# Filler work of an attention and MLP block put in another order within four slots

## The chip, the cores and the metric

The kernel runs on one core of one Trainium2 chip. The metric is the device time of one execution in microseconds. Three runs of the kernel before took 985.18, 988.05 and 989.5 us; their median is 988.05 us.

## The reference

For eight rows b of 512 tokens with 256 features the reference computes a transformer block in fp32. `x` is normalised and modulated (`h`). The attention is the sum of two paths: a light one on all tokens (layer norm, projections q, k, v of 8 heads of 64, each window of 64 tokens attending to itself and its two neighbours, output product `wo_l`), and a heavy one on 256 routed tokens:

```
idx = argsort(scores)                 # scores = h . rt_q and h . rt_kv
rq, rkv = the last 256 rows by each of the two orders
hq = rms(rq) @ wq_h ; hk, hv = split(rms(rkv) @ wkv_h)
ho = softmax(hq hk^T / 8) hv @ wo_h   # written back to the rows of rq
x = x + ga * (light_out + heavy_out)
h = layernorm(x) * (1 + cb) + sb
x = x + gb * spikes(square(relu(h @ W_fc^T)) @ W_proj^T)
```

`spikes` counts, over five steps of a leaky integrator, how often it fires; the kernel does this with five thresholds.

## The kernel before

Each engine has an instruction list written out by hand, and semaphores join them. The work is a pipeline over b = 0 to 7. An iteration has 24 slots: 16 of light attention (4 pairs of heads x 4 tiles of 128 queries) and 8 of heavy attention. In slot s TensorE issues `scores` for the attention step two ahead, then the filler units of the slot, then `turn` (four transposes of the probabilities of this slot) and `attend` for the slot before (lines 1074 to 1083). ScalarE does, in this order, the copy of the transposed probabilities, exp for the step two ahead, its share of the units, and the normalisation for the step one ahead (lines 848 to 860). VectorE copies out the step two back, inverts a row sum, takes the row minimum of the step two ahead, does its share of the units, and last the stages of the slot (lines 1380 to 1395). So on every engine the units come behind the softmax work of the slot. POOL (GpSimd) and SP (the queue that starts the direct DMAs) walk through the slots in the same way.

`SLOT_UNITS` (lines 59 to 84) says which filler units stand in which slot, in order. The units that matter here:

- HT r transposes the routed rows of order r (0: queries, 1: keys and values) into `hT`. ScalarE makes the high part with two activations (line 792), VectorE the low part with two subtractions (line 1318), and the last of these frees the bank.
- HO t is the output product of the heavy path of the row before, four matmuls for each of two tiles. It needs `hoT`, which VectorE completes in slot 1 (line 1300). VectorE multiplies the result by the gate (line 1335), SP stores it, and POOL gathers it back in the order of the tokens in slot 3 (line 635). VectorE adds these rows in slot 5 (line 1245), takes their statistics (lines 1251, 1256), POOL makes the root, and VectorE normalises in slot 6 (line 1264).
- Z3 k transposes the normalised rows; ScalarE modulates and frees the bank (line 776), VectorE splits the result into a high and a low part (lines 1227, 1230), which FC reads.
- HV t is the projection of the routed rows to v; VectorE copies it and frees the bank (line 1313). It is read first in slot 16.
- FC i and YA i are the two products of the MLP. RK r sums the comparisons to ranks (20 small matmuls), which VectorE casts (line 1326) and POOL's scatters read from slot 14 on. SR r transposes the router scores.
- Q, K, V, ZT, HQ, HK, LO and the N-units are further projections and transposes.

All units but YA write to `ps_unit`, which has two banks. They are given in turn, by the place of the unit in the list of its segment (lines 120 and 150 to 160):

```
BANKED = {s: [u for u in units if u[0] != "YA"] for s, units in SEGMENTS.items()}
    i = BANKED[segment].index(unit)
    bank, before = i % BANKS, i // BANKS
```

Before a unit is filled TensorE waits until the last use of its bank has been drained (`fill`, line 881). The segments are `first` (b = 0, without HO, Z3, FC and YA), `loop` (b = 1 to 6), `last` (b = 7, without ZT, SR, RK and the N-units) and a tail with its own list. Those of b = 1 to 6 are called full iterations here.

Of the kernel before, what the change touches and what calls it, by code (L numbers as in the profile page):

```python
# [57 lines left out]

SLOT_UNITS = {
    0: [("HT", 0), ("V", 3)],  # L60
    1: [("HO", 0), ("HO", 1)],
    2: [("HT", 1), ("Q", 2)],
    3: [("HV", 1)],
    4: [("K", 2)],
    5: [("Q", 3)],
    6: [("K", 3)],
    7: [("HV", 0), ("Z3", 0), ("Z3", 1)],
    8: [("FC", 0), ("FC", 1)],
    9: [("HQ", 0), ("FC", 2), ("YA", 0)],
    10: [("FC", 3), ("YA", 1), ("SR", 0)],  # L70
    11: [("FC", 4), ("YA", 2)],
    12: [("FC", 5), ("YA", 3), ("HK", 0)],
    13: [("RK", 0), ("FC", 6), ("YA", 4), ("SR", 1)],
    14: [("FC", 7), ("YA", 5)],
    15: [("YA", 6), ("ZT", 0)],
    16: [("YA", 7), ("ZT", 1), ("RK", 1)],
# [1440 lines left out]
```

## Time and profile before

| | |
|---|---|
| median of 3 runs | 988.05 us |
| profiled execution | 984.39 us |
| its span, first to last instruction | 982.7 us |
| TensorE matmuls busy | 879.1 us (89%) |
| ScalarE busy | 617.0 us (63%) |
| VectorE busy | 552.5 us (56%) |
| GpSimd busy | 402.6 us (41%) |
| mean granted TensorE clock | 0.969 |

The span lies within the time of the execution, which has 1.7 us around it. Busy shares are averages over the whole kernel. An engine that has nothing to do costs time only where another engine, in the end TensorE, waits for it.

### The profile page before, as it was taken

To read this page: it belongs to the slowest core of one execution; us is meant where nothing else is said; L and a number is where in the kernel's file an instruction comes from. 1 tells how busy PE (TensorE), PEld (TensorE's weight loads), DVE (VectorE), ACT (ScalarE), POOL (GpSimd) and SP (SyncE) were. 2 spreads that over 40 slices of the span, in tenths; PEclk is the share of its full clock that TensorE was granted. 3 is DMA by queue.
4 is the path that set the end of the run, shared out by engine and by line. 5 is a ranking of instruction groups with operands and counts; after the bars stand their busy time and mean duration, and the time that the engine had idled before them with its cause. 6 is when DMAs were issued, how large, how long until landed. Compare 5 with 4: busy or idle time off the path is not lost.

```text
span 982.7 us, 19077 instructions
## 1 busy us (share of the span) xinstructions
PE 879.1 (89%) x6866; PEld 674.1 (69%) x6866; DVE 552.5 (56%) x1556; ACT 617.0 (63%) x1682; POOL 402.6 (41%) x453
## 2 busy tenths in 40 slices
PE   5759689899998999899999999899999999999655
PEld 2436567678766877678766877678766877688455
DVE  7645644764557454764557464764557454613344
ACT  1167666676567766676567766676567766777332
POOL 4422040364525453364525453365525443252333
PEclk7989899999999999999999999999999999999968
DMA  9120002100220012200220012200220011200100
GB/s 320 67 81 1 25 31 70 60 1 13 68 84 23 1 39 86 59 2 12 74 79 22 2 38 87 60 2 12 76 76 23 2 38 55 60 2 1 39 22 22
DMA packets 32461, 45.06 MB, mean 46 GB/s; under 512 B 3928, under 2 KB 26720, under 8 KB 32368
## 3 DMA queue, kind: packets, MB, share of 16 engines
q1 hardware_dynamic: 26944, 31.24, 9.9%
q0 software_dynamic: 4608, 12.59, 3.9%
q8 instruction: 56, 0.92, 0.4%
q14 instruction: 37, 0.30, 0.1%
q10 hardware_dynamic: 816, 0.00, 0.0%
HBM read 28.85 MB, written 14.97 MB: 45 GB/s over the span
## 4 chain that ended last, share of the span: by engine, by line
PE 64%; DVE 21%; ACT 6%; issue 4%; POOL 2%; DMA 2%; SPq 1%; DVEq 0%; POOLq 0%; ACTq 0%
PE ps_unit L889 25%; PE ps_y L1000 9%; PE ps_oT L1069 7%; PE ps_unit L937 6%; PE ps_pT L1045 5%; PE ps_scores L1033 4%; PE ps_scores L1025 3%; DVE row_min L1289 3%; PE ps_unit L942 3%; ACT probs L828 3%; DVE late L1215 1%; DVE hT L1318 1%; DVE bn L1251 1%; ACT hT L792 1%; DVE hn L1264 1%
## 5 line engine op out<-in xcount | busy, mean ns | idle before, releaser
L828 ACT ACTIVATE probs<-ps_scores,row_min 128x256 f32<-128x256 f32 (+1 forms) x384 | 171.9, 453 | 133.7 <-DVE row_min L1289 133.6
L839 ACT ACTIVATE probs<-probs,row_inv 128x256 f32<-128x256 f32 (+1 forms) x384 | 166.1, 485 | 0.0
L846 ACT ACTIVATE probsT<-ps_pT 128x512 f32<-128x512 f32 x192 | 113.5, 591 | 41.7 <-PE ps_oT L1069 41.7
L1289 DVE TENSOR_REDUCE row_min<-ps_scores 128x2 f32<-128x384 f32 (+1 forms) x192 | 122.3, 637 | 23.6 <-PE ps_scores L1033 10.8
L1045 PE MATMUL ps_pT<-ident,probs 128*128 128x128 f32 x768 | 116.4, 274 | 3.1 <-ACT probsT L846 2.9
L889 PE MATMUL ps_unit<-xT,wfcT 128*128 128x512 f32 (+1 forms) x432 | 106.1, 386 | 7.3 <-DVE xT L1230 6.7
L889 PE MATMUL ps_unit<-xT,wqkv 128*128 128x512 f32 x384 | 108.6, 419 | 4.0 <-POOL xT L651 4.0
L1300 DVE COPY loT<-ps_oT 128x128 f32<-128x128 f32 x128 | 36.3, 283 | 132.2 <-PE ps_oT L1069 132.2
L428 POOL TENSOR_TENSOR hid<-hid 128x512 f32<-128x512 f32 (+1 forms) x64 | 63.3, 989 | 107.9 <-ACT hid L805 106.9
L1045 PEld LDWEIGHTS ps_pT<-ident,probs 128*128 128x128 f32 x768 | 93.0, 141 | 19.3 <-issue 3.5
L1000 PEld LDWEIGHTS ps_y<-wprojT,hid_parts 128*128 128x128 f32 x768 | 99.8, 191 | 9.1 <-issue 5.2
L1000 PE MATMUL ps_y<-wprojT,hid_parts 128*128 128x256 f32 x768 | 105.2, 285 | 0.2
L889 PEld LDWEIGHTS ps_unit<-xT,wfcT 128*128 128x128 f32 x432 | 73.6, 194 | 29.3 <-issue 17.7
L574 POOL TENSOR_SCALAR veps<-mv 128x4 f32<-128x4 f32 (+1 forms) x25 | 5.1, 204 | 215.1 <-DVE mv L1147 125.0
L889 PEld LDWEIGHTS ps_unit<-xT,wqkv 128*128 128x128 f32 x384 | 70.7, 191 | 24.9 <-issue 10.9
L432 POOL TENSOR_TENSOR hid_parts<-hid,hid_parts 128x512 fp32r<-128x512 f32 (+1 forms) x64 | 78.1, 1220 | 22.0 <-ACT hid_parts L809 20.4
L1069 PE MATMUL ps_oT<-probsT,v 128*64 128x128 f32 x1024 | 85.5, 288 | 0.1
L615 POOL DMA_INDIRECT sorted_rows<-hn,rank x64 | 65.4, 1022 | 44.3 <-DVE rank L1326 31.7
L1025 PE MATMUL ps_scores<-kT,qT 64*64 64x192 f32 (+1 forms) x1024 | 71.3, 336 | 6.7 <-ACT probs L828 5.6
L828 ACT ACTIVATION_READ_ACCUMULATOR probs<-ps_scores,row_min 128x1 f32 x384 | 75.8, 197 | 0.0
L1069 PEld LDWEIGHTS ps_oT<-probsT,v 128*64 128x64 f32 x1024 | 54.2, 137 | 22.0 <-issue 22.0
L809 ACT ACTIVATE hid_parts<-hid 128x512 fp32r<-128x512 f32 (+1 forms) x72 | 42.0, 584 | 42.5 <-PE ps_y L1000 42.0
(157 smaller groups left out, 1508.6 us busy)
## 6 DMA issues: line engine op xcount, KB each, us to landing
xa<-in_L_attn_x SPq DMA_DIRECT2D x8, 512.0 KB, 4.9
routed<-sorted_rows SPq DMA_DIRECT2D x16, 256.0 KB, 2.9
lx<-in_L_attn_x SPq DMA_DIRECT2D x8, 512.0 KB, 3.9
out_x<-spikes SPq DMA_DIRECT2D x16, 256.0 KB, 2.9
routed_out<-late SPq DMA_DIRECT2D x8, 256.0 KB, 2.1
full<-mod_rows SPq DMA_DIRECT2D x7, 256.0 KB, 5.0
sorted_rows<-hn,rank POOLq DMA_INDIRECT x64, 2.4
gate_a<-mod_rows SPq DMA_DIRECT2D x8, 128.0 KB, 3.5
```

The lines of the kernel that those rows point to most:

```text
L428: eng.tensor_tensor(square, hid_relu[:, i % 2, cols], hid_relu[:, i % 2, cols], ALU.mult).then_inc(squared, 1)
L432: eng.tensor_tensor(hid_parts[1][:, i % 2, cols], square, hid_parts[0][:, i % 2, cols].bitcast(F32), ALU.subtract).then_inc(low, 1)
L615: pool.indirect_dma_start(out=sorted_rows[r], out_offset=bass.IndirectOffsetOnAxis(ap=rank[:, r, t:t + 1], axis=0), in_=hn[:, t, :], in_of ...
L828: ins = act.activation(probs[:, probs_buffer(s), h * SEL + lo:h * SEL + hi], ps_scores[:, h, base + lo:base + hi], ACT.Exp, bias=row_min[: ...
L839: ins = act.activation(part, part, ACT.Identity, scale=row_inv[:, s % 3, h:h + 1])
L846: act.activation(probsT[:, :], ps_pT[:, :], ACT.Copy).then_inc(pT_copied, 1)
L889: ins = pe.matmul(ps, w(wi, k, w_cols), a(ai, k, a_cols), start=(n == 0), stop=(n == 3 * KD - 1))
L1000: ins = pe.matmul(ps_y[t // 2][:, (t % 2) * D:(t % 2 + 1) * D], hid_parts[hi][:, i % 2, t * P:(t + 1) * P], wprojT[wi][:, f, :], start=(f ...
L1025: ins = pe.matmul(ps_scores[w * W:(w + 1) * W, h, lo:hi], qT[heads[h], p % 2, query:query + W], kT[heads[h], p % 2, first_key:first_key + ...
L1045: ins = pe.transpose(ps_pT[:, (2 * t + h) * P:(2 * t + h + 1) * P], probs[:, probs_buffer(s), h * SEL + t * P:h * SEL + (t + 1) * P], iden ...
L1069: ins = pe.matmul(ps_oT[h * DH:(h + 1) * DH, 0:P], values[t][:, c0:c0 + DH], probsT[:, (2 * t + h) * P:(2 * t + h + 1) * P], start=(t == 0 ...
L1289: dve.tensor_reduce(row_min[:, s % 3, :], ps_scores[:, :, base + lo:base + hi], AX.X, ALU.min).then_inc(min_ready, 1)
```

## The change

Four slots get another order. In slot 1 the transposes HT 1, which stood first in slot 2, now stand ahead of the heavy output products HO 0 and HO 1. In slot 7 the Z3 transposes stand ahead of HV 0. In slot 13 RK 0 stands behind FC 6 and YA 4. As the list is the same for all engines, each engine's share of these units moves too, and the turn of the banks follows the new order. No unit is added, dropped or changed.

```diff
 SLOT_UNITS = {
     0: [("HT", 0), ("V", 3)],
-    1: [("HO", 0), ("HO", 1)],
-    2: [("HT", 1), ("Q", 2)],
+    1: [("HT", 1), ("HO", 0), ("HO", 1)],
+    2: [("Q", 2)],
     3: [("HV", 1)],
     4: [("K", 2)],
     5: [("Q", 3)],
     6: [("K", 3)],
-    7: [("HV", 0), ("Z3", 0), ("Z3", 1)],
+    7: [("Z3", 0), ("Z3", 1), ("HV", 0)],
     8: [("FC", 0), ("FC", 1)],
...
-    13: [("RK", 0), ("FC", 6), ("YA", 4), ("SR", 1)],
+    13: [("FC", 6), ("YA", 4), ("RK", 0), ("SR", 1)],
```

## Rows read from the trace of the kernel before

**Rows 1.** The page, part 1: busy us, share of the span, instructions.
```profile
PE 879.1 (89%) x6866; PEld 674.1 (69%) x6866; DVE 552.5 (56%) x1556; ACT 617.0 (63%) x1682; POOL 402.6 (41%) x453
```

**Rows 2.** What TensorE waited for: us in total, times, longest.
```profile
PE ps_unit L952 <- DVE v_r L1313: 11.3, 7, 1.8
...
PE ps_unit L942 <- DVE late L1300: 7.2, 8, 1.0
...
PE ps_unit L889 <- DVE hT L1318: 4.3, 6, 0.7
```

**Rows 3.** Timeline, slots 0 and 1 of b = 5: start, us, work, [idle before].
```profile
608.95 0.88 DVE L1318 SCALAR_TENSOR_TENSOR hT<-ps_unit,gamma_cols,hT 128x256 fp32r<-128x256 f32 x2 [1.90 <-ACT hT L792]
...
610.34 0.28 DVE L1300 COPY late<-ps_oT 128x128 f32<-128x128 f32 x1
...
610.76 3.69 PE L942 MATMUL ps_unit<-wo_heavy,late 128*128 128x256 f32 x16 [0.97 <-DVE late L1300]
...
611.99 0.90 ACT L839 ACTIVATE probs<-probs,row_inv 128x256 f32<-128x256 f32 x2
...
614.29 0.60 PE L1045 MATMUL ps_pT<-ident,probs 128*128 128x128 f32 x4
```

**Rows 4.** Timeline, slots 2 and 3 of the same iteration.
```profile
615.41 0.55 PE L1025 MATMUL ps_scores<-kT,qT 64*64 64x128 f32 x8
...
615.89 0.42 PEld L918 LDWEIGHTS ps_unit<-ident,routed 128*128 128x128 f32 x4 [0.27 <-issue]
...
618.29 0.84 ACT L792 ACTIVATE hT<-ps_unit,gamma_cols 128x256 fp32r<-128x256 f32 x2
...
618.89 0.56 PE L1025 MATMUL ps_scores<-kT,qT 64*64 64x192 f32 x8
...
619.24 0.88 DVE L1318 SCALAR_TENSOR_TENSOR hT<-ps_unit,gamma_cols,hT 128x256 fp32r<-128x256 f32 x2 [1.79 <-ACT hT L792]
...
620.17 1.67 PE L889 MATMUL ps_unit<-wkv_r,hT 128*128 128x512 f32 x6 [0.72 <-DVE hT L1318]
```

**Rows 5.** Timeline, the gathered rows and their addition, slots 3 to 5.
```profile
625.31 0.53 POOL L623 COPY rank_kept<-rank 128x4 int32<-128x4 int32 x1 [1.93 <-DMA hn<-routed_out,rank_kept]
...
627.23 1.22 DVE L1245 TENSOR_TENSOR x<-lx,hn 128x1024 f32<-128x1024 f32 x1
```

**Rows 6.** Timeline, slots 6 to 8 of the same iteration.
```profile
632.04 1.38 DVE L1264 TENSOR_SCALAR hn<-x,mv,rstd 128x256 f32<-128x256 f32 x4 [0.93 <-POOL rstd L576]
...
632.81 1.66 PE L889 MATMUL ps_unit<-wkv_r,hT 128*128 128x512 f32 x6
...
634.31 0.60 PE L952 MATMUL ps_unit<-ident,hn 128*128 128x128 f32 x4
...
635.23 0.78 ACT L776 ACTIVATE full<-ps_unit,shift_b,scale_b 128x512 f32<-128x512 f32 x1
...
639.55 3.05 PE L889 MATMUL ps_unit<-xT,wfcT 128*128 128x512 f32 x12 [0.64 <-DVE xT L1230]
```

**Rows 7.** Timeline, the rank sums in slot 13 of the same iteration.
```profile
665.48 0.17 PEld L974 LDWEIGHTS ps_unit<-ones_bf,late 128*128 128x128 bf16 x4 [0.28 <-issue]
```

**Rows 8.** Timeline, slots 6 to 8 of the last iteration, b = 7.
```profile
851.86 1.39 DVE L1264 TENSOR_SCALAR hn<-x,mv,rstd 128x256 f32<-128x256 f32 x4 [0.95 <-POOL rstd L576]
...
855.05 1.51 ACT L776 ACTIVATE full<-ps_unit,shift_b,scale_b 128x512 f32<-128x512 f32 x2
855.09 0.66 PE L952 MATMUL ps_unit<-ident,hn 128*128 128x128 f32 x4 [0.35 <-DVE v_r L1313]
...
858.22 3.05 PE L889 MATMUL ps_unit<-xT,wfcT 128*128 128x512 f32 x12 [0.97 <-DVE xT L1230]
```

**Rows 9.** Timeline, HV 1 in the first iteration, b = 0.
```profile
72.61 2.93 PE L889 MATMUL ps_unit<-wkv_r,hT 128*128 128x512 f32 x6 [2.89 <-DVE wkv_r L1345]
```

**Rows 10.** Busy us by stretch: PE, PEld, DVE, ACT, POOL; granted clock; DMA share, GB/s.
```profile
72.60:73.60 1.00, 0.98 (x2) 0.83 (x3) 0.82 (x3) 0.15 (x1) 0.00 (x0) 0.50 0.00 0
...
500.00:610.00 110.00, 105.60 (x844) 81.67 (x844) 65.47 (x187) 74.98 (x206) 50.71 (x55) 1.00 0.13 42
```

## The prediction

> **What bounds the kernel now.** I began with the engine shares of the page [rows 1]: TensorE is busy 879.1 of 982.7 us, far more than any other. A change that only reorders work can win nothing but TensorE's idle time, so the second view was the list of what TensorE waited for [rows 2]. The reader is to see three entries there that belong to the slots touched: Z3 waits for VectorE's copy of the routed V (11.3 us, 7 times), HO for VectorE's copy into `hoT` (7.2, 8 times, one of them in the tail), HV 1 for the low part of hT (4.3, 6 times, once in each full iteration). Third came the timeline of one full iteration (b = 5), then the places where the last and the first iteration differ. In the timeline each wait ends with a drain on ScalarE or VectorE, engines that run a fixed list of their own; and `ps_unit` has only two banks, handed out in turn in the order of the list. The change reorders the list, so it reorders the banks too, and that decides the sum.
>
> **Slots 1 to 3 of a full iteration.** New order: HT 0 (bank 0), V 3 (1), HT 1 (0), HO 0 (1), HO 1 (0), Q 2 (1), HV 1 (0). No instruction is added or removed.
>
> HT 1 is four transposes paced by their weight loads, 0.42 us [rows 4]. Moved ahead of HO 0 it needs bank 0, which HT 0's subtraction frees at 608.95 + 0.88 = 609.83 [rows 3]; with 0.05 for passing it on (620.12 to 620.17 [rows 4]) it runs from 609.88 to 610.30. HO 0 still needs the copy into `hoT`, which ends at 610.62, and starts at 610.76 as now. So HT 1 is hidden by that wait, and slot 2 is 0.42 shorter.
>
> The price is a new wait. HO 1 fills bank 0 behind HT 1, and HT 1's drain stands behind the softmax in ScalarE's list: in slot 1 ScalarE leaves exp at 611.99 [rows 3]. From there to VectorE's start it takes 0.95 (618.29 to 619.24 [rows 4]), the subtractions take 0.88 and passing on 0.05: HO 1 can start at 613.87. HO 0 is half of the matmuls between 610.76 and turn's start at 614.29 [rows 3], 1.77 us, so TensorE is ready at 612.53 and stands 1.34 us. Behind HO 1 on TensorE are turn(1), attend(0) and the scores of slot 2; on HO 1 itself wait VectorE's second `ho` drain, then stats1, and SP's store of `ho`. Nothing hides this. Bounds: below, 0.72, what HV 1 waits today for the same drain [rows 4]; above, 1.90, the longest VectorE waits for such activations in a full iteration [rows 3]. I take 1.34, as it is worked out in this very slot.
>
> In return HV 1's wait goes. The scores before it start at 618.89; a unit follows scores by 0.48 (615.41 to 615.89), so it could start at 619.37 instead of 620.17 [rows 4]: 0.80. Next in line to be late is exp(4), which those scores need: it ends at 618.29, and TensorE would come at 618.89 - 0.42 = 618.47, just behind it. From HV 1 on VectorE's row of work (v_r copy, center, modulate, x + rows, norm) sets the pace and keeps its distance to HV 1. Slots 1 to 3: +1.34 - 0.42 - 0.80 = +0.12 us.
>
> SP and POOL: the store of `ho` and the four gathers move 1.34 later. Today the gathered rows are there at 625.31 and the addition starts at 627.23 [rows 5]; since the addition moves by only 0.12, its slack shrinks from 1.92 to 0.70 and still hides them. Without that cover the excess would go straight into Z3.
>
> **Slot 7.** New order: Z3 0 (bank 0), Z3 1 (1), HV 0 (0), FC 0 (1). Today HV 0 runs from 632.81, Z3 0 from 634.31 [rows 6], Z3 1 waits 1.8 for HV 0's bank, whose copy stands behind VectorE's stats2 [rows 2], and FC 0 starts at 639.55 after another 0.64 [rows 6]. After: Z3 0 needs the third norm, 632.04 + 1.38 = 633.42, so it starts at 633.47 and not 632.81: a new wait of 0.66. With 0.43 each, Z3 1 is done at 634.33. HV 0 then needs bank 0, freed by ScalarE's activation of Z3 0; that stands behind exp(9) and runs 635.23 to 636.01 [rows 6] wherever Z3 0 lies. HV 0 starts at 636.06, a wait of 1.73, and takes 1.50. From turn to the next unit it is 1.60 (614.29 to 615.89 [rows 3, 4]), so FC 0 starts at 639.16; the h2 parts are there by about 638.3 (cast 0.4 and subtraction 0.7 for each half from 636.05). Gain: 639.55 - 639.16 = 0.39. The waits are moved, not removed. Bounds of the wait before HV 0: 0.35, Z3 1's wait in the last iteration [rows 8], and 1.84.
>
> **Slot 13.** Rank sums 0 start at 665.48 with 0.28 of issue before them and no wait [rows 7], so putting FC 6 and YA 4 ahead wins nothing. VectorE waits some 3 us longer for the rank cast, but its list holds nothing else in that slot, and POOL's scatters start only in slot 14. Cost 0; bounds one issue gap of 0.28 an iteration either way.
>
> **The iterations that differ.** Last (b = 7): HO 1 waits the same 1.34 and slot 2 gives 0.42 back, but HV 1 has no wait to lose. Slot 7 has no stats2 there; Z3 1 waits only 0.35 and FC 0 starts at 858.22 [rows 8]. After: ScalarE's two Z3 activations, 1.51 in all, start at 855.05, so HV 0 can start at 855.05 + 0.77 + 0.05 = 855.87, turn at 857.37, FC 0 at 858.97: +0.75. Together +1.7. First (b = 0): no HO and no Z3. HT 1 is hidden in slot 1, but its subtraction now stands before VectorE's stats1, and the weight subtractions, the copy and the minimum of slot 2 come after; I follow them to HV 1 at about 73.0 instead of 72.61 [rows 9]: +0.4.
>
> **Sum.** Six full iterations x (+0.12 - 0.39) = -1.6; last +1.7; first +0.4: +0.5 us. The profiled execution took 984.39 us (span 982.7 and 1.7 around it), so it would become 984.9. It lies 3.7 below the median of the runs, 988.05; by that median the forecast is **988.6**, practically unchanged. The wait of HO 1 between its bounds, over seven iterations, moves this by -4.3 to +3.9; the wait before HV 0 by -9.7 to +0.8, the low end only if ScalarE took Z3 0 before its exp, which its list forbids.
>
> **The clock.** Over 500 to 610 us, with all of today's waits in it, the granted clock is 1.00 (2.4 GHz). In the first iteration it fell to 0.50 (1.2 GHz) after TensorE had stood still for 2.9 us [rows 10], and HV 1 took 2.93 us [rows 9] instead of 1.66. In the new slot 7 two waits, 0.66 and 1.73, stand with only 0.86 us of transposes between them: thinner than anything in a full iteration now. The Trainium skill (TensorE: Matmul & The Clock Gate, "A second HAM failure mode: psum-queue depth-cycling") says that a kernel cycling through PSUM banks, idling briefly between groups of matmuls, can swing between half and full clock. Today's trace does not agree: two banks in turn, waits of 0.6 to 1.8 us, clock 1.00. By the trace nothing is added; by the rule it would end near 1000.
>
> **Rivals.**
> - *The waits really go.* If HO 1 found its bank free, six full iterations give 1.61 each, the last still costs 0.4 and the first 0.4: -8.9, **979**. For it: HO 0 and HO 1 run today without a gap. Against: the bank turn puts HO 1 behind HT 1, and ScalarE comes to HT 1 only after exp. 0.10.
> - *Slower, the clock.* It falls in slot 7 with the second wait, and HV 0, turn, attend and scores run at 1.2 GHz. Price by the first iteration: 2.93 - 1.66 = 1.3 for HV 0 and some 0.4 more, 1.7 x 7 = 12, **1000**; decided when 0.86 us of transposes between the waits are too little. Only some iterations: 3 to 6 us. 0.12 for both.
> - *Slower, the gathers.* They need more than the 0.70 left, and Z3 0 waits for them; 0.7 of excess in seven iterations is +5, **993.5**. Against: today they keep 1.92. 0.05.
> - *Forecast*, waits moved but not removed: 0.73, its own range 985 to 992.
>
> 0.5% (4.9 us) is about what a measurement of this kernel tells from no change. The range of 983 to 994 leaves out the first rival and the full clock. Faster 0.11, same 0.75, slower 0.14.
>
> **What would show it.** Right: TensorE's wait before HO 0 shrinks to about 0.5, and one of 1.3 appears inside HO, ended by VectorE's hT; none at HV 1 in slot 3; in slot 7 a wait of 0.6 to 0.7 for the third norm, then 1.7 for ScalarE's Z3 activation, and FC 0 without one. Wrong: HO 0 and HO 1 in one run, a half clock in slot 7, or over 1 us before Z3 0.

## The result, and the profile after

The changed kernel takes 996.87 us (median of 7 runs, 993.83 to 999.96), the kernel before in the same comparison 987.81 us (7 runs, 985.18 to 989.5): a ratio of 1.0099, 95% interval 1.0082 to 1.0115. It is slower by 9 us, outside the range of 983 to 994. The profiled execution took 996.87 us, its span is 995.1 (before 982.7), so between these two executions there are 12.4 us to be found.

Part 1 of the page after answers to [rows 1]; below it what TensorE waited for (us in total, times, longest), to [rows 2].

```profile
PE 894.6 (90%) x6866; PEld 681.4 (68%) x6866; DVE 554.7 (56%) x1556; ACT 616.5 (62%) x1682; POOL 401.7 (40%) x453
```

```profile
PE ps_unit L952 <- DVE hn L1264: 17.8, 8, 12.8
PE ps_unit L889 <- ACT full L776: 10.4, 8, 1.4
...
PE ps_unit L942 <- DVE hT L1318: 7.9, 7, 1.1
...
PE ps_unit L942 <- DVE late L1300: 2.1, 8, 0.5
```

The first line holds the surprise: the same 6866 matmuls kept TensorE busy 15.5 us longer, while the span grew by only 12.4. A wait adds nothing to the busy time; matmuls that take longer do. The wait list looks as forecast: HO's wait for the copy has gone from 7.2 to 2.1, one of 1.1 for the low part of hT has come seven times, HV 1's wait and the one for the routed V are gone, and the activation of Z3 is waited for seven times in the loop and the last iteration.

Timeline after, slots 1 to 3 of b = 5, against [rows 3, 4] (start, us, work, [idle before]):

```profile
615.49 1.97 PE L942 MATMUL ps_unit<-wo_heavy,late 128*128 128x256 f32 x8 [0.23 <-DVE late L1300]
...
617.42 0.91 ACT L839 ACTIVATE probs<-probs,row_inv 128x256 f32<-128x256 f32 x2
617.65 0.88 DVE L1318 SCALAR_TENSOR_TENSOR hT<-ps_unit,gamma_cols,hT 128x256 fp32r<-128x256 f32 x2 [1.78 <-ACT hT L792]
618.58 1.99 PE L942 MATMUL ps_unit<-wo_heavy,late 128*128 128x256 f32 x8 [1.12 <-DVE hT L1318]
...
625.11 1.68 PE L889 MATMUL ps_unit<-wkv_r,hT 128*128 128x512 f32 x6
```

HO 1 starts 3.09 us after HO 0; half of HO is 1.77, so TensorE stands 1.32 (forecast 1.34). Slot 7 of two iterations tells the rest. First b = 6, against [rows 6]:

```profile
752.41 1.06 PE L952 MATMUL ps_unit<-ident,hn 128*128 128x128 f32 x8 [0.69 <-DVE hn L1264]
754.06 1.45 ACT L776 ACTIVATE full<-ps_unit,shift_b,scale_b 128x512 f32<-128x512 f32 x2
...
754.89 1.65 PE L889 MATMUL ps_unit<-wkv_r,hT 128*128 128x512 f32 x6 [1.42 <-ACT full L776]
...
756.38 0.60 PE L1045 MATMUL ps_pT<-ident,probs 128*128 128x128 f32 x4
756.91 0.66 PE L1069 MATMUL ps_oT<-probsT,v 128*64 128x128 f32 x8
757.50 0.56 PE L1025 MATMUL ps_scores<-kT,qT 64*64 64x192 f32 x8
757.99 2.36 PE L889 MATMUL ps_unit<-xT,wfcT 128*128 128x512 f32 x9
```

Then the same slot of b = 5, one iteration earlier:

```profile
633.10 1.23 DVE L1245 TENSOR_TENSOR x<-lx,hn 128x1024 f32<-128x1024 f32 x1 [0.84 <-issue]
633.21 1.17 POOL L623 COPY rank_kept<-rank 128x4 int32<-128x4 int32 x1 [3.68 <-DMA hn<-routed_out,rank_kept]
...
639.45 1.06 PE L952 MATMUL ps_unit<-ident,hn 128*128 128x128 f32 x8 [0.89 <-DVE hn L1264]
...
641.93 2.93 PE L889 MATMUL ps_unit<-wkv_r,hT 128*128 128x512 f32 x6 [1.43 <-ACT full L776]
...
644.66 1.06 PE L1045 MATMUL ps_pT<-ident,probs 128*128 128x128 f32 x4
645.65 1.12 PE L1069 MATMUL ps_oT<-probsT,v 128*64 128x128 f32 x8
646.70 0.92 PE L1025 MATMUL ps_scores<-kT,qT 64*64 64x192 f32 x8
```

The order and the waits are the same, but HV 0 takes 2.93 instead of 1.65, `turn` 1.06 instead of 0.60. The windows (PE, PEld, DVE, ACT, POOL busy; granted clock; DMA share, GB/s), to be held against [rows 10], show the clock:

```profile
640.00:641.50 1.50, 0.51 (x5) 0.27 (x3) 1.47 (x5) 1.31 (x5) 0.00 (x0) 0.90 0.00 0
641.50:643.00 1.50, 1.06 (x3) 0.88 (x4) 1.35 (x7) 1.50 (x4) 0.73 (x2) 0.50 0.02 5
643.00:645.00 2.00, 2.00 (x7) 1.52 (x6) 1.20 (x4) 0.23 (x1) 1.65 (x4) 0.50 0.00 0
...
749.00:759.00 10.00, 7.89 (x64) 5.64 (x63) 8.72 (x31) 6.60 (x19) 4.63 (x8) 1.00 0.15 50
```

In b = 5 it falls from 1.00 to 0.50 (2.4 to 1.2 GHz) in the second wait of slot 7 and is back at 1.00 at 648.0 us; in b = 6 it stays. The duration of HV 0 tells which iterations were hit: 2.52 in b = 1, 2.67 in b = 3, 2.93 in b = 5; 1.65 to 1.68 in b = 2, 4, 6 and 7.

**Where the 12.4 us are.** The start of HO 0 marks the iterations. Before: 169.33 for b = 1, 831.57 for b = 7, and 110.3 to 110.4 for each iteration between ([rows 3] have the start of b = 5, 610.76). After: 171.43, 283.25, 393.50, 505.28, 615.49, 729.40, 839.70, which is 111.82, 110.25, 111.78, 110.21, 113.91, 110.30. So
- an iteration at full clock is 0.1 to 0.2 us shorter than before; the sum said 0.27;
- one with a half clock in slot 7 takes 1.5 to 1.6 more than that. In b = 5 the half clock lasts longer (from Z3 0 to the next HO 0 89.95 us, 87.2 at full clock: 2.7 more), and its late addition of the gathered rows puts 0.9 on top (from HO 0 to Z3 0 23.96 us instead of 23.03). The six together: +6.0;
- the stretch ahead of b = 1's HO 0 is 2.1 longer (forecast +0.4), that behind b = 7's HO 0 4.3 longer (forecast +1.7).

### The profile page after: what moved, and what is told of

The parts are those of the page before. It is cut to its first block, busy times and chain, and to the rows that moved or that the text cites. A ratio compares the mean times of both kernels' runs of the same rounds, so it can differ in the third digit from the quotient of the medians.

```text
span 995.1 us, 19077 instructions
## 1 busy us (share of the span) xinstructions
PE 894.6 (90%) x6866; PEld 681.4 (68%) x6866; DVE 554.7 (56%) x1556; ACT 616.5 (62%) x1682; POOL 401.7 (40%) x453
## 4 chain that ended last, share of the span: by engine, by line
PE 67%; DVE 17%; ACT 6%; issue 5%; POOL 2%; DMA 1%; ACTq 0%; DVEq 0%; SPq 0%; POOLq 0%
PE ps_unit L889 27%; PE ps_y L1000 8%; PE ps_oT L1069 8%; PE ps_pT L1045 6%; PE ps_unit L937 6%; PE ps_scores L1025 4%; PE ps_scores L1033 4%; ACT probs L828 3%; DVE row_min L1289 3%; PE ps_unit L942 1%; DVE late L1215 1%; DVE hT L1318 1%; ACT hT L792 1%; DVE bn L1251 1%; DVE hn L1264 1%
## 5 line engine op out<-in xcount | busy, mean ns | idle before, releaser
L1045 PE MATMUL ps_pT<-ident,probs 128*128 128x128 f32 x768 | 119.1, 279 | 3.5 <-ACT probsT L846 3.5
L1045 PEld LDWEIGHTS ps_pT<-ident,probs 128*128 128x128 f32 x768 | 95.6, 144 | 21.2 <-issue 4.7
L428 POOL TENSOR_TENSOR hid<-hid 128x512 f32<-128x512 f32 (+1 forms) x64 | 63.5, 993 | 113.4 <-ACT hid L805 112.4
```

Of the source, the lines that this page charges most:

```text
L428: eng.tensor_tensor(square, hid_relu[:, i % 2, cols], hid_relu[:, i % 2, cols], ALU.mult).then_inc(squared, 1)
L1045: ins = pe.transpose(ps_pT[:, (2 * t + h) * P:(2 * t + h + 1) * P], probs[:, probs_buffer(s), h * SEL + t * P:h * SEL + (t + 1) * P], iden ...
```

## The experiments

Each kernel was timed in five rounds against the kernel before on the same chip; ratios have their 95% interval. Two theories stood against each other. *The clock*: new waits in slot 7 let it fall in some iterations. *The waits themselves*, or gathers that are late in most iterations: a fixed price for each iteration.

**Each slot alone.**

```diff
-    1: [("HO", 0), ("HO", 1)],
-    2: [("HT", 1), ("Q", 2)],
+    1: [("HT", 1), ("HO", 0), ("HO", 1)],
+    2: [("Q", 2)],
```

> Only the edit of slots 1 and 2: HT 1 ahead of HO 0 and HO 1. Theory A (the change is neutral at full clock; what was lost is TensorE's clock, above all in slot 7): no half clock in slot 7; per full iteration +0.2 us as in the changed kernel's trace (HO 1 waits 1.3, HV 1 no longer), last +1, first +0.4 at full clock plus some 1.7 if its gaps again cost a second stretch of half clock there: +3 to +5 us in all. Rival B (the new bank waits themselves are the loss, and slots 1 to 3 have the longest of them over seven iterations): +7 us or more. Rival C (the late gather, as in iteration 5 of the changed kernel, is a frequent loss and not a single one): the addition of the gathered rows waits in most iterations, +5 or more.

993.2 us (990.82 to 995.15), ratio 1.0057 (1.0041 to 1.0072). This part does cost, and the surprise is where. An iteration at full clock takes 110.6, 0.2 more than before. In slot 7, which still has the old order and where the expectation had no half clock, TensorE's clock fell in b = 4 and b = 6 (iterations of 112.4 and 112.6); in just these two the addition came late. Timeline of b = 4:

```profile
518.93 1.23 DVE L1245 TENSOR_TENSOR x<-lx,hn 128x1024 f32<-128x1024 f32 x1 [0.79 <-issue]
519.04 1.17 POOL L623 COPY rank_kept<-rank 128x4 int32<-128x4 int32 x1 [3.63 <-DMA hn<-routed_out,rank_kept]
...
528.45 0.66 PE L952 MATMUL ps_unit<-ident,hn 128*128 128x128 f32 x4 [2.05 <-DVE v_r L1313]
```

POOL waits 3.63 us for the landing instead of 1.93 [rows 5], the slack of 0.70 is not enough, and Z3 1's wait grows from 1.84 to 2.05. Before, six waits of 1.81 to 1.84 left the clock alone; with 0.2 more (2.05 and 2.03) it fell, both times.

```diff
-    7: [("HV", 0), ("Z3", 0), ("Z3", 1)],
+    7: [("Z3", 0), ("Z3", 1), ("HV", 0)],
```

> Only the edit of slot 7: Z3 0 and Z3 1 ahead of HV 0. Theory A: at full clock -0.4 per full iteration and +0.75 in the last, -1.6 us in all; but two waits of 0.7 and 1.4 us with 0.9 us of transposes between them make the granted clock fall to half in about half of the iterations, 1.5 us each: +2 to +5 us over the kernel before. Rival B (waits alone): -1.6 us, and no iteration at half clock would then matter. First iteration and the heavy slots before the tail as in the kernel before.

989.85 us (987.5 to 991.66), ratio 1.0013 (1.0001 to 1.0026). The gain at full clock is there (171.41 to 281.42 is 110.0, from 110.4), and in b = 2, 4 and 6 the half clock takes it back (iterations of 111.5 to 111.6):

```profile
747.27 1.06 PE L952 MATMUL ps_unit<-ident,hn 128*128 128x128 f32 x8 [0.69 <-DVE hn L1264]
749.76 2.44 PE L889 MATMUL ps_unit<-wkv_r,hT 128*128 128x512 f32 x6 [1.43 <-ACT full L776]
752.00 1.05 PE L1045 MATMUL ps_pT<-ident,probs 128*128 128x128 f32 x4
```

```diff
-    13: [("RK", 0), ("FC", 6), ("YA", 4), ("SR", 1)],
+    13: [("FC", 6), ("YA", 4), ("RK", 0), ("SR", 1)],
```

> Only the edit of slot 13: RK 0 behind FC 6 and YA 4. Both theories: no change, within 1 us of the kernel before, because RK 0 has no wait today. If the three edits do not add up (slots 1 and 2 alone +5.0, slot 7 alone +1.7, all three +9.2), this one would have to be worth +2.5 us for Rival B to stand; under theory A the missing part is the clock, which more waits in one iteration lower more often.

989.11 us (986.65 to 992.93), ratio 0.9993 (0.9977 to 1.0009): nothing, as forecast. Its trace has iterations of 110.6 to 110.7, though, 0.3 longer than before. Most of that comes from slot 4, which has the same order in both: VectorE's copy out of `ps_oT` begins 0.2 to 0.3 late there. In slot 13 TensorE loses nothing.

**The change again**, beside the first two on their chip.

> The changed kernel once more, on the chip of the others, with a second profile. Theory A: again +9 us; slots 1 to 8 of an iteration that keeps its clock take the same time to 0.1 us, but which iterations fall to half clock may differ from the first trace, as the clock's own timing is not tied to the kernel. If the loss were a fixed wait (Rival B), the same iterations would be long by the same amounts.

997.39 us (993.76 to 1003.02), ratio 1.0107 (1.0077 to 1.0137). This time the half clock was in b = 1, 3 and 6 and late additions in b = 5 and 6. Which iterations are hit differs from execution to execution. The kernel's times spread over 9 us, those of the kernel before over 6 in the same comparison.

In b = 5 of this execution the late addition stands alone:

```profile
633.32 1.23 DVE L1245 TENSOR_TENSOR x<-lx,hn 128x1024 f32<-128x1024 f32 x1 [1.23 <-issue]
...
642.16 1.66 PE L889 MATMUL ps_unit<-wkv_r,hT 128*128 128x512 f32 x6 [1.43 <-ACT full L776]
```

HV 0 runs at full clock, and the iteration takes 111.56 instead of 110.25: a late addition costs 1.3 by itself.

**Work in the gap.** The change as it is, and 14 transposes of finished probabilities between Z3 1 and HV 0, where TensorE stands.

```diff
+            def keep_busy(n, s):
+                pe.wait_ge(probs_ready, n + 1)
+                pe.wait_ge(pT_copied, n)
+                for i in range(14):
+                    pe.transpose(ps_pT[...], probs[...], ident[:, :])
...
                     for u in slot_units(s, first, last):
+                        if s == 7 and not first and u == ("HV", 0):
+                            keep_busy(n, s)
                         unit(segment, b, u)
```

> The changed kernel, with 14 more transposes of the probabilities into the bank that turn overwrites, put into TensorE's list of slot 7 between Z3 1 and HV 0 (1.5 us of work in a wait of 1.55 us; results not used). Theory A: the wait is filled with activity, the clock in slot 7 stays at 2.4 GHz in every iteration, HV 0 takes 1.66 us each time, and although 98 instructions are added the kernel gets faster than the changed one by about 5 us (+3 to +5 over the kernel before instead of +9). Rival B (the bank waits are the loss, whatever the clock does): the wait only changes its name, the time stays at +9 or rises.

987.06 us (985.16 to 990.89), ratio 0.9991 (0.9976 to 1.0005): with 98 instructions more, 10 us less than the change on the same chip. Timeline of b = 5:

```profile
635.32 1.06 PE L952 MATMUL ps_unit<-ident,hn 128*128 128x128 f32 x8 [0.69 <-DVE hn L1273]
636.22 1.69 PE L1054 MATMUL ps_pT<-ident,probs 128*128 128x128 f32 x14
637.80 1.67 PE L889 MATMUL ps_unit<-wkv_r,hT 128*128 128x512 f32 x6
```

HV 0 starts no earlier: 2.48 us after Z3 0, as in b = 5 and 6 of the change. It only runs at full clock, in every iteration, and each iteration takes 110.23 to 110.35, which is what the change takes where its clock holds. This time no addition was late, so the 10 us contain that too: the loop of the profiled after_again is 7.0 longer than this one, 4.5 of it in the three half clocks and 2.6 in the two late additions.

**The same work where no clock falls.** The order of before, with the 14 transposes between Z3 0 and Z3 1, in its wait of 1.84.

> The order of before in all slots; in slot 7 (b = 1 to 7) 14 more transposes of finished probabilities stand between Z3 0 and Z3 1, in the wait of 1.8 us for HV 0's bank. Their result is not used. The clock theory: before has no half clock in that slot, so there is nothing to give back, and the transposes fit into the wait (14 x 0.13 = 1.8 us): 986 to 990 against 988, ratio 0.998 to 1.002. The rival, that the 14 transposes gained 10 us in the new order by something else (a shifted start, another pairing of the loads), expects a gain here as well, 3 us or more. If the transposes are longer than the wait, some 0.2 an iteration, +1.4.

989.81 us (985.87 to 990.73), ratio 0.9999 (0.9982 to 1.0015). Here, where no clock falls and no addition is late, the transposes give nothing.

**How much work.** `range(4)` and `range(8)` instead of `range(14)` in the change.

> The order of the change with 4 instead of 14 transposes put between Z3 1 and HV 0 in slot 7 (b = 1 to 7; their result is not used). They take some 0.5 of the 1.4 to 1.7 us for which TensorE waits before HV 0. The clock theory has no number for the amount of work that is needed: if 0.5 us of work in the gap is enough, all half clocks between the first iteration and the tail are gone and the time is 986 to 989, as with 14 (ratio 0.998 to 1.001); if it is not, some iterations keep it, 990 to 997, and HV 0 shows 2.4 to 2.9 us in those. The rival, that the change costs its time elsewhere, expects 996 to 998 in both cases.

994.82 us (992.74 to 995.86), ratio 1.0055 (1.0037 to 1.0073), and a finding neither theory had. All seven HV 0 take 1.66 or 1.67 us, the clock holds in the whole loop with 0.5 us of work in the wait; by the expectation that meant 986 to 989. But each full iteration takes 111.3 or 111.4. Timeline of slots 4 and 5, b = 5:

```profile
630.84 0.15 DVE L1303 RECIPROCAL row_inv<-row_sum 128x2 f32<-128x2 f32 x1
...
631.99 0.69 DVE L1298 TENSOR_REDUCE row_min<-ps_scores 128x2 f32<-128x512 f32 x1 [1.00 <-remote]
...
633.79 0.56 PE L1025 MATMUL ps_scores<-kT,qT 64*64 64x192 f32 x8 [1.25 <-ACT probs L828]
```

VectorE is free at 630.99 and the scores that it needs were done at 629.93, yet the minimum starts at 631.99; exp follows late, and TensorE waits 1.25 us for it.

> The order of the change with 8 transposes put between Z3 1 and HV 0 in slot 7 (b = 1 to 7; their result is not used). With 4 of them no half clock was left in the loop, but the time was 994.8: in slot 5 of each full iteration the scores waited 1.25 us for exp, because VectorE's minimum of slot 4 began 1.0 us after both its scores and the work before it were done. With 14 that stall was not there. The clock theory: the half clocks are gone here too, and what remains depends on that stall alone: without it 985 to 989 (ratio 0.998 to 1.001) and iterations of 110.2; with it 993 to 996 and iterations of 111.3. The rival, that 4 transposes left part of the change's own cost standing, expects a time between the two (989 to 993) with iterations of an even 110.7.

994.92 us (992.46 to 997.19), ratio 1.0067 (1.0041 to 1.0093), iterations of 111.3 to 111.4, HV 0 at 1.64 to 1.67 in all of them, the same stall in each full iteration: the second branch of the expectation. Of the rival's iterations of 110.7 nothing is seen. What sets off the stall isn't settled. It is in neither kernel of the comparison nor in those with 14 transposes, it is in those with 4 and 8, and in all three that follow with both HO products in one bank. In before_busy_gap, hv_in_slot8 and slot13_only VectorE's copy out of `ps_oT`, two instructions ahead of this minimum, begins 0.1 to 0.3 late, perhaps a small form of the same. Where the stall is, the minimum begins 0.8 to 1.0 us behind the end of POOL's fourth gather issue; but the change issues that gather at the same place and has no stall. The kernel with the 4 transposes, then, holds its clock beside a stall that the change doesn't have.

**Taking the waits away.** HV 0 moves out of slot 7 altogether, all else as before:

```diff
-    7: [("HV", 0), ("Z3", 0), ("Z3", 1)],
-    8: [("FC", 0), ("FC", 1)],
+    7: [("Z3", 0), ("Z3", 1)],
+    8: [("HV", 0), ("FC", 0), ("FC", 1)],
```

> The kernel before, with HV 0 moved from slot 7 to the head of slot 8, so that the scores, turn and attend stand between the Z3 transposes and HV 0. Theory A: the only waits left are 0.7 for the third norm and under 1 us before FC 0, no half clock in slot 7, FC 0 some 1.3 us earlier in a full iteration: -5 to -8 us against the kernel before, 980 to 983 us. Rival B (a wait for a bank costs its length wherever it stands): HV 0 still waits for ScalarE's drain of Z3 0, and the gain is under 2 us.

983.06 us (981.64 to 983.96), ratio 0.9926 (0.9909 to 0.9944). Timeline of b = 5:

```profile
630.67 1.06 PE L952 MATMUL ps_unit<-ident,hn 128*128 128x128 f32 x8 [0.68 <-DVE hn L1264]
631.58 0.60 PE L1045 MATMUL ps_pT<-ident,probs 128*128 128x128 f32 x4
632.11 0.66 PE L1069 MATMUL ps_oT<-probsT,v 128*64 128x128 f32 x8
632.69 0.56 PE L1025 MATMUL ps_scores<-kT,qT 64*64 64x192 f32 x8
633.18 1.65 PE L889 MATMUL ps_unit<-wkv_r,hT 128*128 128x512 f32 x6
635.51 1.88 PE L889 MATMUL ps_unit<-xT,wfcT 128*128 128x512 f32 x7 [0.68 <-DVE xT L1230]
```

Z3 stands ahead of HV 0 as in the change, but the softmax work of slot 8 lies between them: two waits of 0.68 in place of 0.7 and 1.4, an iteration of 109.4 to 109.5, and no half clock in the loop. FC 0 starts 27.84 us behind HO 0, 0.95 earlier than before (the expectation had 1.3).

For slots 1 and 2, both HO products in the two halves of one bank with one drain, so that no bank has to come round:

```diff
-    1: [("HO", 0), ("HO", 1)],
-    2: [("HT", 1), ("Q", 2)],
+    1: [("HT", 1), ("HP", 0)],
+    2: [("Q", 2)],
...
+                elif kind == "HP":
+                    pe.wait_ge(oT_copied, SLOTS * b)
+                    for t in range(2):
+                        for p in range(PAIRS):
+                            ins = pe.matmul(ps[:, t * D:(t + 1) * D], ...)
```

> The edit of slots 1 and 2 with the wait of HO 1 taken away: both heavy output products fill the two halves of one bank as one unit behind HT 1, and VectorE drains them in one instruction. Theory A and the bank reading of slot 1: no wait inside HO, HT 1 hidden, no wait at HV 1: -1.2 us per full iteration, +0 to +2 in the first iteration, -4 to -7 us in all; the gathered rows have 1.2 us less slack and may come late in some iterations, which would show as VectorE waiting before the addition and would eat 1 to 2 us each. If the 1.3 us wait in slot 1 is not what the edit costs, this is no faster than slots 1 and 2 alone (+5).

990.62 us (988.54 to 993.33), ratio 0.9997 (0.9984 to 1.0011), and not the 4 to 7 us less that were expected. HO runs without a gap, and the stall of the minimum takes the gain; besides, the clock fell in the old slot 7 of b = 3 and b = 4, behind waits of 1.86 and 1.85, and held behind one of 1.89. The stall in b = 2:

```profile
294.23 0.69 DVE L1298 TENSOR_REDUCE row_min<-ps_scores 128x2 f32<-128x512 f32 x1 [1.15 <-remote]
...
296.02 0.56 PE L1034 MATMUL ps_scores<-kT,qT 64*64 64x192 f32 x8 [1.40 <-ACT probs L831]
```

> Both of the last two together. If they touch different waits, their differences add: -9 to -14 us, 974 to 979 us, with no half clock between the first iteration and the tail. If VectorE's work from HV 1 to the third norm sets the pace of these slots, or the gathered rows come late, the sum stays at the better of the two.

980.02 us (978.72 to 982.4), ratio 0.9894 (0.9876 to 0.9913): the best version, 1.06% faster than the kernel before and just behind the expected 974 to 979, with the stall still in it. In b = 5 the rows landed late here too (POOL waits 4.03), as in b = 5 of ho_pair (3.74); neither addition had to wait for them.

> The fastest order so far (both HO products in one bank behind HT 1 in slot 1, HV 0 in slot 8) with 4 transposes put before FC 0 in slot 8, in a wait of 0.67 us (their result is not used). It has the same stall of VectorE's minimum in slot 4 (1.1 us in each iteration). If the stall hangs on how TensorE's instructions lie in an iteration, four more may move it away: 8 iterations x 1.1 to 1.4 less, 969 to 972. If it hangs on the order of the units or on VectorE's own list, which are unchanged, it stays: 979 to 982, ratio 0.989 to 0.992.

981.93 us (978.31 to 984.42), ratio 0.9926 (0.9897 to 0.9955). The stall stays in every iteration (0.97 to 1.11), so more work on TensorE doesn't move it away.

## Why the prediction was wrong

Right at full clock, step by step:
- HT 1 is hidden: HO 0's wait shrank to 0.23 behind HT 1 (about 0.5 was forecast). HO 1's wait: 1.32 for 1.34. HV 1 has none left.
- Slot 7: 0.69 for 0.66; the second wait 1.62, counted as in the forecast (2.48 between the starts of Z3 0 and HV 0, less twice 0.43), for 1.73. FC 0 comes without a wait.
- The full iteration: 110.2 to 110.3 from 110.3 to 110.4, -0.12 on average for -0.27. Slots 1 to 3 cost 0.22 for 0.12, slot 7 gives 0.39 for 0.39. Slot 13: nothing.
- The last iteration: +1.8 for +1.7 in after_again, where its clock held.
- With the wait before HV 0 filled, the time was 987.06, ratio 0.9991: close to the "practically unchanged" of the forecast.

**The step that failed** is the one on the clock: "By the trace nothing is added". That the clock was 1.00 with today's waits was read as room for more, and there was none: waits of 1.85 to 2.05 in the old slot 7 lost the clock four times out of seven in the two orders that had them, and in the new slot 7 the waits of 0.7 and 1.4 us with the Z3 transposes between them lost it in three of seven iterations in each of three executions. The price was about right (1.4 to 1.6 us in eight of these nine iterations and 2.7 in the ninth, for 1.7; "only some iterations: 3 to 6 us", and the three in the profiled change cost 5.9), the chance of 0.12 was not: it came in every profiled execution with this slot 7 and nothing in the wait, though the prediction had itself called the pair of waits "thinner than anything in a full iteration now". The Trainium skill's rule (TensorE: Matmul & The Clock Gate, "A second HAM failure mode: psum-queue depth-cycling"), set aside there by the row of 1.00, is what this trace after agrees with: from 1.00 to 0.50 and back, between groups of matmuls that wait for a bank.

**What no rival held** is the other half, 6.4 us outside the six full iterations. Most of it is not shown to be the change's. In the first iteration HV 1 was forecast at 73.0. It came there in slots12_only, and b = 1's HO 0 at 169.56, +0.2 for the forecast +0.4; in the change it came at 73.81. HV 1 in slots12_only:

```profile
73.00 2.93 PE L889 MATMUL ps_unit<-wkv_r,hT 128*128 128x512 f32 x6
```

But the changed execution was behind before it came to the first unit that was moved (HT 1, at 64.35). The turn ahead of it, first before, then in the change, then in slot7_only, whose first iteration is that of before:

```profile
62.19 0.60 PE L1045 MATMUL ps_pT<-ident,probs 128*128 128x128 f32 x4
```

```profile
62.51 1.05 PE L1045 MATMUL ps_pT<-ident,probs 128*128 128x128 f32 x4
```

```profile
62.37 1.05 PE L1045 MATMUL ps_pT<-ident,probs 128*128 128x128 f32 x4
```

The half clock of this stretch ended at about 61.8 us before and at about 64.3 in the other two. Three kernels with the first iteration of before (slot7_only, slot13_only, before_busy_gap) reach b = 1's HO 0 at 171.41, 172.03 and 171.35, like the change with 171.43. So the 1.7 beyond the forecast are no more than executions with the same first iteration differ by, and the 169.33 of the profiled kernel before is the low end.

Behind b = 7's HO 0, 1.7 was forecast and 4.3 measured. In slots 21 to 23, which the change doesn't touch and whose waits are as before, the clock was at half here:

```profile
931.28 1.06 PE L1045 MATMUL ps_pT<-ident,probs 128*128 128x128 f32 x4 [0.85 <-ACT probsT L846]
932.27 1.12 PE L1069 MATMUL ps_oT<-probsT,v_r 128*64 128x128 f32 x8
934.14 1.12 PE L1069 MATMUL ps_oT<-probsT,v_r 128*64 128x128 f32 x8 [0.76 <-ACT probsT L846]
935.75 4.87 PE L942 MATMUL ps_unit<-wo_heavy,late 128*128 128x256 f32 x16 [0.48 <-DVE late L1300]
```

The same four groups take 0.63, 0.66, 0.66 and 3.69 us before: 2.5 of the missing 2.6. The HO of the tail ran partly at half clock (4.6 to 5.0 us) in seven of the fourteen profiled executions, before_busy_gap, which has the order of before, and hv_in_slot8 among them, and not in after_again. So nothing shows it as a cost of the new order.

**The gathers** are a second step that failed, a smaller one. The slack shrank as computed (0.69 in b = 1), and it was judged enough at a chance of 0.05. In three executions with HO 1 behind HT 1 the landing came too late once, twice and twice; in the three with transposes in the gap, never. Each late one cost 0.6 to 1.3 us up to Z3 0, 1.3 in the iteration that had no half clock beside it. Part of the 1.0057 of slots 1 and 2 is this. What delays the landing, and whether the transposes have a part in its absence, stays open.

## What to carry to other kernels

When a busy engine's order is changed, look at how the waits lie to each other, not only at their sum: a granted clock of 1.00 beside the waits of today doesn't show that a little more is free. Two waits that come close together deserve a price at half clock and nearly an even chance (here 9 of 21 iterations), and what is cheap to try is to put the next slot's softmax work between them, or useless transposes into the longer one. Profile a kernel more than once before a difference in a stretch that the change doesn't touch is put down to the change. Of two banks handed out in turn, a unit put ahead of another takes the other's bank: moving the consumer a slot on (0.7%) was worth more than the reordering within the slot.

## What the runs showed of the hardware

- The granted clock fell around waits of 0.7 and 1.4 us with the eight Z3 transposes between them, in 3 of 7 iterations in each of three executions; it didn't fall once where 4, 8 or 14 transposes filled part or all of the second wait (21 iterations), and not in the loop with two waits of 0.68. Which iterations are hit changes with the execution. Single waits of 1.80 to 1.84 in slot 7 never did it (17 in four orders); of seven of 1.85 to 2.05 four did, and it isn't the length alone: 1.86 lost it, 1.89 did not.
- The time from the gathers' last issue to their landing varies: POOL waits 1.9 to 2.6 us as a rule, 3.6 to 4.1 in seven late cases, all of them in orders with HT 1 in slot 1.
- VectorE can start a minimum 0.9 to 1.15 us after both its input and its last instruction are done, at the same place in each full iteration of five kernels. It cost 1.1 us an iteration; its cause is open.
